# Two graph-attention layers on one core: converting two adjacency load slots with one VectorE instruction

## The reference

```python
h = relu(layernorm(x))
Wh = h @ W
e = leaky_relu((Wh @ a1)[:, None] + (Wh @ a2)[None, :], 0.2)
scores = where(adj > 0, e, -9e15)
x = x + elu(softmax(scores, axis=1) @ Wh)
```

## Time and profile before

| | |
|---|---|
| median of three runs | 1382.87 us |
| the profiled execution | 1382.77 us |
| its span in the trace | 1381.1 us |
| busy in the span | DVE 89%, ACT 86%, TensorE 84%, POOL 22% |
| groups 0 to 13 of the first layer | 107.6 to 710.8 us of the span |
| groups 14 and 15 | 710.8 to about 790 us |
| DMA engines, first 21 of 40 slices | 90% busy or more |

### The profile page before, as it was taken

How to read it: one execution, slowest core, us unless ns; L and a number is a source line. 1 busy time by engine, 2 the same in 40 slices (tenths; PEclk the granted TensorE clock), 3 DMA queues, 4 the chain that set the end, 5 groups by cost and what they waited for, 6 DMA issues and landing times. The chain is left out here.

```text
span 1381.1 us, 52802 instructions
## 1 busy us (share of the span) xinstructions
PE 1155.4 (84%) x20824; PEld 1122.3 (81%) x20824; DVE 1226.5 (89%) x2207; ACT 1191.2 (86%) x1829; POOL 308.9 (22%) x520
## 2 busy tenths in 40 slices
PE   2727988989989897899998761999899989999996
PEld 2427988988989887898988750999899989998996
DVE  7688989998999988889998878889999989998996
ACT  2248999999999998999999735999999989998995
POOL 2343444444454543344420000000000000000000
PEclk9958999999999998999999976999999999999998
DMA  9999999999999999999982000000101010010000
GB/s 159 174 196 196 210 198 209 211 212 211 206 212 207 212 210 206 177 194 211 209 170 56 9 22 31 2 26 3 33 2 32 2 33 9 25 32 3 18 2 24
DMA packets 128142, 157.24 MB, mean 114 GB/s; under 512 B 59280, under 2 KB 59408, under 8 KB 128016
## 3 DMA queue, kind: packets, MB, share of 16 engines
q0 software_dynamic: 73728, 134.25, 52.9%
q1 hardware_dynamic: 54288, 21.11, 7.0%
HBM read 285.25 MB, written 4.26 MB: 210 GB/s over the span
## 5 line engine op out<-in xcount | busy, mean ns | idle before, releaser
L1232 PE MATMUL psum<-parts_d,toggle 128*128 128x130 f16 x8192 | 985.8, 223 | 39.0 <-DVE work L972 36.6
L1232 PE MATMUL psum<-parts_g,work 128*128 128x130 f16 x8192 | 985.4, 222 | 0.1
L1232 PEld LDWEIGHTS psum<-parts_d,toggle 128*128 128x128 fp8e4 x8192 | 805.5, 99 | 44.5 <-issue 44.2
L1232 PEld LDWEIGHTS psum<-parts_g,work 128*128 128x128 fp8e4 x8192 | 812.2, 99 | 6.2 <-issue 2.3
L565 ACT ACTIVATE toggle<-s_row,steep_d 128x512 uint8 (+1 forms) x952 | 590.8, 727 | 0.7
L565 ACT ACTIVATE toggle<-stream,steep_d 128x1024 uint8<-128x1024 f32 x419 | 443.4, 1155 | 27.8 <-PE psum L1232 27.8
L655 POOL DMA_DIRECT2D stream<-in_adj_dram x512 | 307.6, 603 | 385.6 <-DVE stream L718 327.6
L967 DVE TENSOR_TENSOR toggle<-work,toggle 128x1024 int32<-128x1024 int32 x256 | 312.4, 1220 | 68.7 <-ACT toggle L565 65.8
L972 DVE TENSOR_TENSOR work<-work,toggle 128x1024 int32<-128x1024 int32 x256 | 311.9, 1218 | 0.8
L718 DVE TENSOR_SCALAR stream<-stream 128x1024 bf16<-128x1024 bf16 x512 | 201.4, 422 | 34.5 <-DMA stream<-in_adj_dram 27.5
L1126 PE MATMUL psum<-pack_w,stream 128*128 128x8 bf16 x4096 | 131.9, 166 | 73.5 <-DVE stream L718 59.4
(11 more groups left out here) (119 smaller groups left out, 372.7 us busy)
## 6 DMA issues: line engine op xcount, KB each, us to landing
stream<-in_adj_dram POOLq DMA_DIRECT2D x512, 256.0 KB, 7.7
s_row<-s_scratch SPq DMA_DIRECT2D x16, 256.0 KB, 6.0
stream<-s_scratch SPq DMA_DIRECT2D x8, 512.0 KB, 4.3
toggle<-in_x_dram SPq DMA_DIRECT2D x4, 512.0 KB, 6.9
x_tile<-in_x_dram SPq DMA_DIRECT2D x16, 128.0 KB, 10.6
x_scratch<-y_tile SPq DMA_DIRECT2D x16, 128.0 KB, 9.5
stream<-x_scratch SPq DMA_DIRECT2D x4, 512.0 KB, 5.4
stream<-x_scratch SPq DMA_DIRECT2D x8, 256.0 KB, 4.3
```

What stands on the lines that cost most here:

```text
L1232: ins = nc.tensor.matmul(psum[:, bank, COLS[third]:COLS[third + 1]], mask.bitcast(FP8), parts[e][:, t, :, :].rearrange("p k h -> p (k h)") ...
```

## The change

In the groups of the first layer a new function `convert_two` replaces two calls of `convert`. It waits for both load slots and for the packing of both old steps, converts two neighbouring slots (2048 columns) with one instruction, and adds 2 to `conv`. Of a chunk's four steps the first two are converted in `between(0)`, ahead of the AND, none in `between(1)`, and the last two in `between(2)`. The preparation keeps `convert`.

```diff
+            def convert_two(eights, s):
+
+                for k in range(2):
+                    dve.wait_ge(stage_in[(s + k) % STAGES], (eights + (s // STAGES + 1)) * 16)
+                dve.wait_ge(packed, eights * 8 + (s + 2))
+                nc.vector.tensor_scalar(natural[:, s % NAT:s % NAT + 2, :], stage[:, s % STAGES:s % STAGES + 2, :], 0.0, None,
+                                        ALU.is_gt).then_inc(conv, 2)
+
...
                     def between(k):
                         if L == 0:
-                            for s in steps_at(c, limit)[(0, 1, 2)[k]:(1, 2, PACE)[k]]:
-                                convert((g + 1) * (GSTEPS // 8), s)
+                            for s in steps_at(c, limit)[(0, 2, 2)[k]:(2, 2, PACE)[k]:2]:
+                                convert_two((g + 1) * (GSTEPS // 8), s)
                         if not first:
                             finish_between(L, g - 1, c, k)
```

## The result

The changed kernel takes 1396.29 us in the median of eight runs, the kernel before 1383.3: ratio 1.011, 95% interval 1.0073 to 1.0146. It is 13 us slower, where no change was forecast. The two profiled executions (1382.77 and 1399.31 us) differ by 16.5. Groups 0 to 13 start 0.6 us later and end at 730.1 us of the span and not at 710.8: 18.7 us more in them, of which 2.3 come back in groups 14 and 15.

The account below looks back on a forecast made before the run. The prediction took the DMA's loads, at a full 209 GB/s, to set the first layer's group time. The profiled 1382.77 us, plus 1.0 for an offset paid once, minus 0 to 0.3, gave 1384 us; range 1377 to 1397.

Parts of the forecast that it names:

- The instruction: One paired conversion on DVE takes 0.69 us, 0.07 less than two singles; 1.1 us saved a group, worth 0.
- The walk: In one group, from chunk 3's first pair to chunk 4's XOR: that XOR and TensorE's start come 1.0 us later.
- that offset is paid when it first arises and then stays: DVE falls at most about 1.25 us behind the landings, once; each group still takes the loads' 42.3 us.
- The sum: Whole kernel: 1382.77 us, plus 1.0 for the offset paid once, minus 0 to 0.3, gives 1384 us.
- 0 to about 1 us a group: Open bound on the cost in first-layer groups if the DMA loses rate with about two loads in flight.
- 3.3 at the worst: Fewest loads in flight before, of 8 slots: 4.4 us from issue to landing against one load every 1.32 us.
- The late masks are paid in each group: Slower rival at chunk 4: TensorE's and ACT's longer waits cost 14 groups +14 us, half given back +7; chance 0.14.
- The loads are starved behind the unpack: Slower rival: load issues held until the unpack ends, DMA idle 0.6 us; 1391 us, at both unpacks 1400; chance 0.10.
- a DMA share under 1.12: Sign in the groups' profile: with ACT's waits grown, the late masks; unchanged at 1.12 in 42.3 us, the forecast.

Follow-up runs that it names:

- e15: Kernel before with one added DVE memset of 896 fp32 columns ahead of chunk 4's AND in each first-layer group; ratio 1.0111.
- e7: Kernel before, but from the fifth row tile on each load waits for one conversion more than it needs; ratio 1.0177.
- e8: Kernel before, but from the fifth row tile on each load waits for two conversions more than it needs; ratio 1.0503.
- half loads: Kernel before, each load bringing only the first 512 of its 1024 columns, half of the adjacency matrix left out; ratio 0.988, in a second run 0.9859.
- e11: The half loads on the kernel before, first run; ratio 0.988 to the kernel before.
- e17: The half loads on the kernel before, nothing added, run as the base of e16; 1362.32 us, ratio 0.9859 to the kernel before.
- e16: The half loads on the kernel before plus e15's added DVE memset ahead of chunk 4's AND; 1379.89 us, ratio 1.0003 to the kernel before.
- e3: Kernel before, but only the last two steps of a chunk converted as a pair, the first two single where they stood; ratio 1.0003.
- e1: Changed kernel's order with single conversions: two ahead of the AND, two after the XOR; ratio 1.0108 to the kernel before.
- e10: Changed kernel, but chunk 4's first pair stands ahead of the unpack instead of behind it; ratio 1.0157 to the kernel before.
- e13: Changed kernel, but chunk 4's second pair also stands ahead of the AND, right behind the first; ratio 1.0108 to the kernel before.
- e14: Changed kernel with chunk 3's first pair behind its AND and chunk 4's second pair ahead of its AND; ratio 1.0084 to the kernel before.
- e4: Kernel before, but the load into an even slot waits until the odd slot beside it is converted too; ratio 1.0109.

## Why the prediction was wrong

*The instruction* was right: 687 ns against 0.69 us, 228 of them, DVE's load down by 0.8 us a group (1.1 forecast), and worth nothing.

*The walk* was right in its mechanism. The first pair of chunk 3 waits for the second landing, the XORs of chunks 3 and 4 come later, TensorE waits longer there (35.0 us for 27.0 over the groups) and so does ACT (37.1 for 26.4). From one XOR to the other the walk gives 7.15 us, and the group shown has 7.17. e15 prices the 1.0 us that the walk had found for chunk 4: 0.81 us of DVE ahead of that AND costs 1.1% on its own.

*The step that failed* is the one after it: "that offset is paid when it first arises and then stays". The sum had 1.0 us for the whole kernel; groups 0 to 13 took 18.7 us more, 1.3 a group. The step took the landings for a fixed line that nothing on DVE can move, on two grounds, and both are wrong.
- The rate was to hold with two or three loads in flight, "0 to about 1 us a group". Rows 3 showed a steady rate only at the depth that the kernel before had, and "3.3 at the worst" is the shortest load's time divided by the mean spacing, which is no count of loads in flight: before, three or fewer were in flight for 4.4% of groups 2 to 13, in the changed kernel for 13.3%. e7 takes a load out of flight and costs 1.8%, e8 5.0%, and the changed kernel shows 166 to 181 GB/s after the unpack. The bound, 14 us in all, stood in the prediction; the value taken was its lower end.
- The DMA was to be the one that sets the pace, so that a delay elsewhere is absorbed. The half loads show a second limit 1 us behind it (1.2 to 1.4% of the time; in e11 most groups take 41.3 or 41.4 us and some 43.3, with all loads 42.0 to 43.2). The waits suggest a ring: from chunk 4's masks through TensorE (20.1 us in e17, 36.3 in e16), its packs and ACT's `store_words` (ACT waits 14.2 and 24.9 us for TensorE) and the signs back to DVE. That it closes in this way is argued from the waits; no run opens it elsewhere. What e15 and e16 do show is that a delay ahead of chunk 4's AND is paid over the groups, whether the DMA is full or not. Its marks stood in rows 7 and 8, TensorE waiting 2.6 us for DVE and ACT 2.06 us for TensorE in the same group.

*The rivals.* "The late masks are paid in each group" named the place and the price (+7 to +14 us; measured +13) and had 0.14. "The loads are starved behind the unpack" had 0.10; its signs are there too, but not by its cause. It had both slots come free right ahead of the unpack, and e3 does just this at no cost (1.0003); here it is the late unpack that frees them late. The sign given for choosing between them, a DMA share under 1.12, did not serve: 1.11 in the changed kernel, and 1.12 in a group of 43.8 us of e1. Two stalls of 1 us in one place, each enough, deserved more than 0.24 together. The range did reach to 1397.

*What stays open.* In the changed kernel chunk 4's masks and the slots released around it come late together, by the same wait. Each costs as much without the other: 1.3% from e17 to e16, without a full DMA, and 1.8% in e7, without anything added on DVE. Their shares in the 13 us were not separated. e10, e13 and e14 moved both, and in e15, whose edit touches no load, three loads or fewer are in flight for 13.7% of the time all the same. Why e4 was slower stays open too.

*The two places from the Trainium skill.* By the practical ceiling that the Trainium skill gives in Perfetto Trace Analysis (Roofline), some DMA rate was to spare; the half loads show that the DMA does cost about 1 us a group at the rate of the rows. POOL's row has four issues in 4.56 us across the unpack and two in 1.19 elsewhere; the rule of the Trainium skill in SBUF — State Buffer (Who interferes with whom), that a DVE instruction which holds the shared ports blocks GpSimd for its whole length, agrees. But e3, where both slots come free right ahead of the unpack, loses nothing, so the rule alone made no difference here.

## What to carry to other kernels

Merging two instructions of an engine into one moves the earlier one's consumers behind the later one's inputs; price that wait at the place where another engine already stands waiting for this one, and take it as paid in each turn of the loop unless something shows that it isn't. An idle share of an engine says nothing of slack at a given point: DVE had 3.3 us idle in the group of rows 6 and, from chunk 3's first conversion to chunk 4's XOR, none. A rate that stays flat shows that a resource is full at the queue depth that it has; before a slot is held longer, measure what one slot less costs. And where a change moves a wait from one instruction to another, add up both before you say that it grew.

## What the runs showed of the hardware

- The DMA's rate depends on the loads in flight. Over stretches of 2 us of groups 2 to 13, in all fifteen traces with full loads, the loads' queue moved 197 and 194 GB/s in the mean with four and five in flight, 187 with three, 134 with two and 109 with one (five stretches).
- Groups of 42.0 to 43.2 us became 43.5 to 44.3 in most with up to one of eight loads less (e7), and 45.4 to 48.6 with up to two less (e8); their late landings delay DVE too. The DMA share hardly shows it (1.12, 1.11, 1.06).
- One conversion of 2048 bf16 columns takes 687 ns, two of 1024 back to back 0.76 us: the pair is worth 0.07 us.
- A memset of 896 fp32 columns took 805 ns.
